# VectorE takes every second turned tile of x out of PSUM, where ScalarE took them all

## The reference

```python
edge_index = jnp.stack([src, dst])
h = jnp.maximum(_layernorm(x, axis=-1), 0.0)
x = x + _L0_gnn_ref(h, edge_index, W1, b1, W2, b2, W3, b3)   # 3 times: h @ W, weighed sum over edges
h = jnp.maximum(_layernorm(x, axis=-1), 0.0)
x = x + _L1_gnn_ref(h, relvectors, w_ih, w_hh, b_ih, b_hh, src, dst, edge_type_16)
```

## Time and profile before

| | us |
|---|---|
| median of 3 runs (lowest, highest) | 858.27 (856.66, 858.71) |
| the profiled execution, its own time | 857.42 |
| its span in the profile | 853.2 |
| TensorE busy | 821.6 |
| VectorE busy | 606.7 |
| ScalarE busy | 297.6 |
| GpSimd busy | 123.8 |

### The profile page before, as it was taken

How to read it: one execution, slowest core, us unless ns; L and a number is a source line. 1 busy time by engine, 2 the same in 40 slices (tenths; PEclk the granted TensorE clock), 3 DMA queues, 4 the chain that set the end, 5 groups by cost and what they waited for, 6 DMA issues and landing times.

```text
span 853.2 us, 14286 instructions
## 1 busy us (share of the span) xinstructions
PE 821.6 (96%) x4710; PEld 465.7 (55%) x4710; DVE 606.7 (71%) x1319; ACT 297.6 (35%) x604; POOL 123.8 (15%) x244
## 2 busy tenths in 40 slices
PE   2889999999999999999999999999999999999997
PEld 1457566666666545445555544555554555455554
DVE  8955999999999265555867546575665656565677
ACT  3365666776777312110101302221202122112233
POOL 0210112013000036655760000000000000000000
PEclk9989999999999999999999999999999999999999
DMA  6100000000000511613301112222704112112232
GB/s 208 33 2 1 4 18 23 16 17 18 24 17 17 171 30 51 183 41 76 76 8 49 59 50 98 87 75 84 201 23 145 38 42 51 28 37 44 56 81 52
DMA packets 89689, 49.83 MB, mean 58 GB/s; under 512 B 52843, under 2 KB 86396, under 8 KB 89612
## 3 DMA queue, kind: packets, MB, share of 16 engines
q1 hardware_dynamic: 73836, 39.00, 16.3%
q10 hardware_dynamic: 15776, 9.85, 4.1%
HBM read 29.68 MB, written 18.78 MB: 57 GB/s over the span
## 4 chain that ended last, share of the span: by engine, by line
PE 89%; DVE 7%; issue 1%; ACT 1%; DMA 1%; SPq 0%; DVEq 0%
PE ps L1396 19%; PE ps L1058 13%; PE ps L1744 11%; PE ps L955 9%; PE ps L1570 9%; PE ps L757 5%; PE ps L764 5%; PE ps L1421 4%; PE ps L1439 3%; PE ps L769 2%; PE ps L774 2%; PE ps L1030 2%; PE ps L986 1%; DVE node_b L298 1%; PE ps L1018 1%
## 5 line engine op out<-in xcount | busy, mean ns | idle before, releaser
L1058 PE MATMUL ps<-node_a,count 128*128 128x512 f16 x525 | 181.0, 381 | 1.5 <-DVE node_a L1165 1.1
L955 PE MATMUL ps<-node_b 128*128 128x175 f16 x808 | 162.2, 256 | 5.5 <-DVE node_b L298 3.5
L298 DVE TENSOR_TENSOR node_b<-node_b 128x1024 f16<-128x1024 f16 (+2 forms) x253 | 157.1, 669 | 0.0
L1254 ACT ACTIVATE count<-ps 128x500 f32 x202 | 122.9, 608 | 65.1 <-PE ps L955 59.4
L1396 PE MATMUL ps<-count,node_a 128*128 128x512 f16 (+2 forms) x686 | 130.7, 351 | 0.0
L2329 POOL TENSOR_TENSOR count<-count,node_a 16x20 f16 x202 | 89.7, 444 | 94.9 <-DMA chapter_starts<-in_dst 53.9
L955 PEld LDWEIGHTS ps<-node_b 128*128 128x128 f16 x808 | 79.5, 100 | 35.0 <-issue 7.0
L1396 PEld LDWEIGHTS ps<-count,node_a 128*128 128x128 f16 (+1 forms) x686 | 60.1, 98 | 69.1 <-issue 0.4
L1744 PE MATMUL ps<-count,node_a 128*128 128x512 f16 x288 | 64.1, 379 | 0.0
L1058 PEld LDWEIGHTS ps<-node_a,count 128*128 128x128 f16 x525 | 53.2, 101 | 18.9 <-ACT count L1254 1.2
L727 ACT ACTIVATE count<-count 128x512 f32<-128x512 f32 (+1 forms) x25 | 15.8, 630 | 118.3 <-DVE count L790 118.3
(11 more groups left out here) (289 smaller groups left out, 1134.0 us busy)
## 6 DMA issues: line engine op xcount, KB each, us to landing
node_a<-in_x SPq DMA_DIRECT2D x4, 768.0 KB, 8.2
second_scratch<-node_a ACTq DMA_DIRECT2D x4, 768.0 KB, 3.8
node_a<-second_scratch ACTq DMA_DIRECT2D x4, 768.0 KB, 4.3
node_b<-second_scratch ACTq DMA_DIRECT2D x8, 384.0 KB, 5.1
state_scratch<-params SPq DMA_DIRECT2D x24, 128.0 KB, 1.9
node_b<-state_scratch SPq DMA_DIRECT2D x96, 32.0 KB, 2.1
table_scratch<-agg SPq DMA_DIRECT2D x21, 128.0 KB, 1.8
mixed_scratch<-node_b SPq DMA_DIRECT2D x10, 256.0 KB, 2.0
```

The costliest lines, as they stand in the source:

```text
L298: return DVE.tensor_tensor(to, iota, keys.unsqueeze(2).to_broadcast([P, n, width, 2]), ALU.is_equal)
L955: return PE.matmul(window(s)[:, :, keys], low, key_hot[k][:, j, :, i].rearrange("p (t w) -> p t w", w=SPAN), start=(s == 0 and j == 0), st ...
L1058: last = PE.matmul(out_slot(u)[0:m, :], count[:, t, u * P:u * P + m], node_a[:, t, :, :].rearrange("p a d -> p (a d)"), start=(t == 0), st ...
L1254: ACTE.activation(to, window(s), ACT.Copy).then_inc(win_written, 1)
```

## The change

For the odd tiles from 9 to 23, eight of the 25, the copy with its relu moves from ScalarE to VectorE, with a semaphore of its own, `x_turned_too`. VectorE does tile t in its beat t + 14, which is `TURN_AT` + `BEATS` behind t. TensorE's waits are shared out between the two semaphores. Nothing else changes. (The new lines shift the numbers of those behind them: 1254 becomes 1267, 1282 becomes 1295, 1287 becomes 1301, and the new copy is line 1122.)

```diff
+        x_turned_too = sem("x_turned_too")
...
+        def copied_by_dve(t):
+            return t > LATER_TURNS and t % 2 == 1
+
+        def copied_at(t):
+            by_dve = copied_by_dve(t)
+            return x_turned_too if by_dve else x_turned_out, sum(copied_by_dve(k) == by_dve for k in range(t + 1))
...
                 if t:
-                    PE.wait_ge(x_turned_out, t if t <= LATER_TURNS else t - 1)
+                    PE.wait_ge(*copied_at(t - 1 if t <= LATER_TURNS + 1 else t - 2))
...
-                    PE.wait_ge(x_turned_out, T)
+                    PE.wait_ge(*copied_at(T - 1))
+                    PE.wait_ge(*copied_at(T - 2))
...
+            t = beat - TURN_AT - BEATS
+            if 0 <= t < T and copied_by_dve(t):
+                DVE.wait_ge(x_turned, t + 1)
+                DVE.tensor_scalar(turned_x(t), turned(t), 0.0, None, ALU.max).then_inc(x_turned_too, 1)
...
-                ACTE.wait_ge(x_turned, t + 1)
-                ACTE.activation(turned_x(t)[:, :, 0:m], turned(t)[:, :, 0:m], ACT.Relu).then_inc(x_turned_out, 1)
+                if not copied_by_dve(t):
+                    ACTE.wait_ge(x_turned, t + 1)
+                    ACTE.activation(turned_x(t)[:, :, 0:m], turned(t)[:, :, 0:m], ACT.Relu).then_inc(x_turned_out, 1)
```

## The result

| | before | after |
|---|---|---|
| median (lowest, highest), us | 858.45 (856.66, 858.71), 4 runs | 868.13 (866.59, 868.97), 4 runs |
| ratio to before, 95% interval | | 1.0122 (1.0110 to 1.0134) |
| the profiled execution, its own time | 857.42 | 868.14 |
| its span in the profile | 853.2 | 864.0 |
| TensorE busy | 821.6 | 825.5 |

The kernel became slower by 1.2%, as forecast (867.0, range 863.0 to 869.5). The quotient of the two medians is 1.0113, 9.7 us.

A forecast was written before the change was run, and what follows sets the result against it. TensorE bounds the kernel (89% of the chain's span), with ScalarE setting the pace from about 52 to 55.4 us. 2.25 + 5.0 + 0.1 + 1.35 = +8.7 us on the median 858.27 gives 867.0, range 863.0 to 869.5.

The forecast's parts named there:

- Pair 2: VectorE's one-hots and key rows of pair 2 stand behind copy 9, so TensorE starts block 4 late: +2.25 us.
- The variance: The variance stands behind copy 11, ScalarE's root behind it, then turn 12: +7.25 us at tile 12, 5.0 of the sum.
- the 0.5 us I gave the clock: Allowance for a lower TensorE clock from block 4 to turn 11, after three idle microseconds; from 0 to 1.0.
- Tiles 12 to 21: Stretch from turn 12 to the end of turn 21: 6.1 us instead of 6.0, between ends of 4.6 and 7.0.
- Pair 3: VectorE's one-hots of pair 3 stand behind copy 21, so TensorE starts block 6 later: +1.35 us, +8.7 in all.
- The histogram: VectorE's root, line 1142, scale steps and copy 23 are just covered by TensorE's work from block 6: no further cost.
- the two margins of 0.2 us: Places at the histogram where TensorE's work only just covers VectorE's, by 0.2 us.
- A: Only the direct waits for pairs 2 and 3 count; TensorE is not held for the root: 861.9 us, chance 0.13.
- C: Not slower: VectorE's waits end in time, ScalarE's relief from 52 to 55.4 us gains 1.1 to 1.4: 857.0, chance 0.04.
- D: A transfer or another engine would have held TensorE anyway: about the same time, 858.3 us, chance 0.04.
- B: The low clock reaches into the first products of x: +1.2 us, 868.2, up to 869.5 if it lasts; chance 0.14.
- The terms of the spread: Uncertainties of the forecast: copies ±0.4 us, clock -0.6, tiles 12 to 21 from -1.5 to +0.9; own range 864.9 to 868.4.

The follow-up runs named there:

- only9: The changed kernel with VectorE copying tile 9 alone and ScalarE the 24 others; 863.76 us, ratio 1.0069.
- turn9_early: The changed kernel with turn 9 waiting for copy 7, as before the change; 866.57 us, ratio 1.0104, and 867.34 us, ratio 1.0113, in a further set.
- before_turn9_late: The kernel before with one number changed: turn 9 waits for the copy of tile 8 and not of tile 7; 860.76 us, ratio 1.0031.
- root24: The changed kernel with ScalarE's root of the variance moved from its beat 16 to its beat 24; 863.66 us, ratio 1.0067.
- variance_first: The changed kernel with VectorE's copy of tile 11 two beats later, behind the variance; 864.19 us, ratio 1.0073.
- behind_early: The changed kernel with its eight VectorE copies behind the one-hots of pair 3, and turn 9 waiting for copy 7 as before; 857.74 us, ratio 0.9994.
- from13: The changed kernel with VectorE copying only tiles 13 to 23 (six), ScalarE also 9 and 11; 860.51 us, ratio 1.0034.
- only9_root24: The changed kernel with VectorE copying tile 9 alone and ScalarE's root in beat 24 instead of 16; 862.46 us, ratio 1.0057.
- after_again: The changed kernel once more, unchanged, as reference in a later set; 866.62 us, ratio 1.0103 to the kernel before.
- behind13_early: As behind_early, but VectorE copies only tiles 13 to 23, and 9 and 11 stay on ScalarE; 857.96 us, ratio 0.9997.

## Why the prediction was right, and where it was not

1. **Pair 2, +2.25.** Measured +2.22, with the wait and its releaser as forecast. only9 shows it alone. The copy's occupancy was 0.34, not 0.40. The 0.78 us for loading registers lie within this wait, as I said, but I had not seen that the change also moves that load. turn9_early against after shows that this costs nothing here, and before_turn9_late that it costs 3 us without the cover (0.31%). "Nothing else changes", in the account of the change, was wrong in this.

2. **The variance, +7.25 in all.** Measured +7.25: the root comes at 56.22, 8.93 us behind the end of turn 9, and I had 8.8 (54.78 less 45.98). root24 and variance_first show both halves of the chain. The agreement to the hundredth is luck. Turn 11 ended 6.9 us behind turn 9 where I had 6.1: two pairs of products and two pairs of transposes at 1.2 GHz cost more than the 0.5 us I gave the clock. Behind copy 11 the way from the start of the one-hot to the end of line 617 was shorter, 1.61 us (54.57 to 56.18) instead of 2.23, line 617 itself 0.18 instead of 0.43; the last section has the likely reason.

3. **Tiles 12 to 21, +0.1.** This step failed by its size: +0.78 (8.03 less 7.25). I took the row's 6.0 us with the engines waiting for each other in turn. But the clock was at 1.2 GHz from 57.6 to 64.4, in which a tile's turn took mostly 0.53 to 0.67 us where it took 0.35 to 0.41, which is more than a relieved ScalarE can give back (0.5 us in behind_early). The upper end I had named, 7.0, was the nearer one: 6.77 were measured.

4. **Pair 3, +1.35.** Measured +1.29, seen again in from13 (2.15 against 0.85). As written, 0.40 and 1.71 give 2.11 and not 2.2; measured were 2.14 (64.69 to 66.83).

5. **The histogram, 0.** Right (9.32 and 9.27). VectorE waits for it 0.22 us, so the two margins of 0.2 us held. One part was read wrongly. VectorE and GpSimd in order of time in the changed kernel,

```profile
59.45 0.18 DVE L1185 TENSOR_REDUCE bounds<-count 128x1 f32<-128x32 f32 x1
...
59.76 0.39 POOL L2324 PARTITION_ALL_REDUCE fours<-bounds  x1 [7.13 <-DVE bounds L1185]
```

GpSimd's reduction comes 0.13 us behind its input, and I had put 5.7 us of delay between them. Those 5.7 us of issue have another cause than VectorE's beat 27, and I expected the reduction at 64.5 instead of 59.76. In all fourteen profiles it starts 5.6 to 7.5 us behind GpSimd's last centring (before 45.68 and 51.39, now 52.63 and 59.76), so the delay seems to count from there; what it is stays open. It did not matter, as it is off the path.

**The rivals.** A fell with root24 and variance_first. C fell with copy 9's wait, and behind_early shows that most of the gain it counted on is not there either. D is excluded by the total. B held in part: the clock was low in the first products until 74.7 us. The first 24 products took 7.00 us from 71.36; before they took 6.89 from 60.78. So they themselves lost only 0.1. Then block 8 waited, in the changed kernel:

```profile
78.97 0.79 PE L963 MATMUL ps<-node_b 128*128 128x175 f16 x3 [0.60 <-issue]
```

It is a register load once more (1.93 us from 76.9 on), which before started at 65.7 and ended ahead of the last product. Why it starts nearer to the end of the products was not tested. This is +0.6 us that no step of mine had.

**The 1.3 us ahead of turn 9** belong to no step either. Tile 8 is turned 1.16 us later in the profile of after (45.90) than in that of before (44.74), and nothing that was changed acts before it; 0.17 more is the later wait of turn 9. The changed kernel's profile is 0.15 us late from the first block on (22.50, before 22.35). Then the clock fell at 30.3 us in it and at 32.2 in the other, and came back 1.5 us later (37.1 and 35.6). In the other profiles turn 9 starts between 45.66 (only9_root24) and 47.03 (variance_first), with the same program up to there. So single profiles can differ by 1.4 us here with nothing changed, mostly by the clock's phase. By the medians the change costs 8.5 us (after_again) to 9.7, and my 8.7 lies within that by its steps, which all count from turn 9. The times on record tie the spread between executions to the clock as well: of the 45 executions of the kernel before that the ranges of the three sets count, the 23 with a mean granted clock of 0.991 took 857.88 to 859.29 us, and the 9 with 0.995 took 856.35 to 858.01.

**The clock as a whole.** The prediction put all of the stretch from 49 us at 1.2 GHz. In the profile of the changed kernel it was not: the level was back at 2.4 GHz from 54.2 to 57.6 and from 64.4 to 67.8, mostly while TensorE stood idle. In that of after_again, the same kernel, it stayed low from about 49.5 to 63.2. Both were at the lower level for 23.9 us in all.

**Small slips.** The forecast without the clock's 0.5 is 8.2 and not 8.1, and 52.1 with a copy of 0.40 is 52.5 and not 52.55. The terms of the spread, simply added, reach from 864.5 to 868.3; 864.9 to 868.4 does not come out of them as written. None of these changes the range or what follows from it.

**No version beats both kernels.** behind_early and behind13_early are level with the kernel before.

## What to carry to other kernels

An engine that works ahead of the others must not be given an instruction that waits for them, unless it is put behind everything that they will need of it. Count the price of such a move as what stands behind the wait, not as the instruction's length: here 0.34 us of work per copy, costing nothing in one place of the queue and 9 us in another. When waits are rewritten, compare the number waited for at each step, one by one; here one copy more to wait for, at one tile, was worth 0.3% by itself. And before relieving a full engine, look for a loop through one buffer that has the same period.

## What was not expected of the hardware

- **Register loads stand in line too.** TensorE's load of offsets (line 534) took 1.07, 1.70 and 1.93 us in three places, started only behind the waits ahead of it in the queue, and shows in the views only as idle time "issue" or under the name of an innocent releaser. It is on the path of blocks 4 and 6 in the kernel before (0.78 and 0.85) and of blocks 4 and 8 in others.
- **A short wait can cost several times its length through the clock.** In before_turn9_late 0.7 us of idle time became 2 us in the profile and 3 by the medians, with pairs of products of 0.87 us instead of 0.53. In the changed kernel the waits of 3.0 and 3.7 us were each followed by a stretch at 1.2 GHz, 23.9 us between 30 and 75 us against 10.2. The Trainium skill, page "TensorE: Matmul & The Clock Gate", section "What's actually happening", has the lower level as the default and activity as what releases it. The trace agrees in part: these stretches follow the waits, but for 3.0 us of the first wait and 3.4 of the second the granted clock was still or again at 2.4 GHz while TensorE did nothing (47.3 to 50.3 and 54.2 to 57.6). The same section calls the number of products at the lower level run-variable, and with this the traces agree: the stretch that begins at 30.3 us in one profile and at 32.2 in the other lasts 6.8 us in the one and 3.4 in the other, with the same program up to there.
- **VectorE and GpSimd took turns in some forms, a whole instruction at a time.** GpSimd in order of time, its centring of three tiles, in the kernel before,

```profile
42.96 2.72 POOL L2308 TENSOR_SCALAR node_a<-node_a,moments 128x256 f32<-128x256 f32 x3 [6.58 <-DVE moments L603]
```

and in the changed kernel:

```profile
50.73 1.90 POOL L2322 TENSOR_SCALAR node_a<-node_a,moments 128x256 f32<-128x256 f32 x3 [14.20 <-DVE moments L603]
```

Of the three tiles only the first differs: 1.80 us beside VectorE's two one-hots (from 42.79 on), 0.99 beside one (50.55), where each of the two others took 0.47 or 0.48 in both. So the first one probably stood waiting until about 44.3 (an estimate: its end, 44.76, less 0.47), behind the one-hots. VectorE's small steps then split in two. Lines 603, 609 and 610, all begun by 44.30, took 0.14, 0.19 and 0.19 us, no longer than in the changed kernel, where GpSimd had long been done (0.15, 0.20, 0.20). Lines 612, 614 and 617 took 0.27, 0.42 and 0.43 against 0.19, 0.18 and 0.18 there. Each of these three ended within 0.05 us of the end of a tile on GpSimd (44.76, 45.22, 45.68). only9_root24 shows the same, shifted by one step:

```profile
50.85 0.43 DVE L610 TENSOR_TENSOR newt<-count 128x25 f32<-128x25 f32 x1
...
51.77 0.42 DVE L614 SCALAR_TENSOR_TENSOR newt<-newt 128x25 f32<-128x25 f32 x1
52.22 0.18 DVE L617 TENSOR_SCALAR newt<-newt 128x25 f32<-128x25 f32 x1
```

There GpSimd's tiles ended at 51.24, 51.70 and 52.16; line 610 is long, line 612 too (0.41), and line 617, behind the last tile, is short. So part of what copy 11's wait cost came back in this way (the 0.6 us of step 2). It does not hold for all forms: elsewhere in the same traces three such tiles took 1.45 us (from 34.93) with VectorE busy nearly all the while, and no kernel was made to test the two engines apart.
